# A state-space layer and expert mix on one core: y and B turned by VectorE, group factors copied by GpSimd

## What is computed

```python
proj = xn @ in_proj_w.T                       # gate (4096), x (4096), B, C (8*128 each), dt (64)
xBC  = silu(causal_conv(proj_xBC, 4 taps) + conv_bias)
# for every head: state = state*exp(dt*A) + (dt*x) B^T ;  y = state C
y    = y + x * D
yn   = y * rsqrt(mean(y*y over a group of 512) + eps) * norm_weight * silu(gate)
out  = x_in + yn @ out_proj_w.T + xn @ W_base.T + b_base + top2_lora(xn)
```

## Time and profile before

| | us |
|---|---|
| median of 3 runs | 3145.19 |
| lowest, highest | 3144.51, 3145.26 |
| profiled execution, device time | 3145.09 |
| its span in the trace | 3143.4 |

### The profile page before, as it was taken

The page is one execution under the profiler, slowest core; times in us unless marked ns, Lnnn a source line. Parts: engine busy times, 40 slices in busy tenths (PEclk is TensorE's granted clock), DMA queues, the critical chain, the costliest instruction groups (busy, mean ns, idle before and its releaser), DMA issues.

```text
span 3143.4 us, 55218 instructions
## 1 busy us (share of the span) xinstructions
PE 3126.1 (99%) x17660; PEld 2573.4 (82%) x17660; DVE 2558.5 (81%) x4599; ACT 1704.5 (54%) x4467; POOL 835.5 (27%) x917
## 2 busy tenths in 40 slices
...
GB/s 290 274 265 272 264 276 266 261 256 263 232 216 194 189 201 187 189 194 201 173 225 205 191 191 191 201 184 190 209 166 236 196 195 187 195 194 201 186 189 161
DMA packets 185668, 672.63 MB, mean 214 GB/s; under 512 B 21056, under 2 KB 22208, under 8 KB 185408
## 3 DMA queue, kind: packets, MB, share of 16 engines
...
...
## 4 chain that ended last, share of the span: by engine, by line
PE 95%; DVE 2%; ACT 1%; DMA 1%; issue 0%; SPq 0%; POOL 0%; ACTq 0%; DVEq 0%; POOLq 0%
PE dense L1072 21%; PE dense L1074 21%; PE dense L1073 21%; PE pX L1072 7%; PE pX L1074 7%; PE pX L1073 6%; PE pY L1187 3%; PE pD L1217 1%; PE pD L1187 1%; DVE conv_us L1497 1%; PE pCB L1163 1%; PE pU L1072 1%; PE pS L1073 1%; PE pS L1072 1%; PE pS L1074 1%; PE pU L1074 1%
## 5 line engine op out<-in xcount | busy, mean ns | idle before, releaser
L1072 PE MATMUL dense<-xn_hi,w_hl 128*128 128x512 f32 (+2 forms) x2192 | 869.7, 397 | 0.8 <-POOL w_hl L444 0.5
L1074 PE MATMUL dense<-xn_hi,w_hl 128*128 128x512 f32 (+2 forms) x2192 | 853.7, 389 | 0.0
L1073 PE MATMUL dense<-xn_lo,w_hl 128*128 128x512 f32 (+2 forms) x2192 | 852.0, 389 | 0.0
L1497 DVE SCALAR_TENSOR_TENSOR conv_us<-conv_in,const_g,conv_us 128x512 f32<-128x512 f32 x576 | 480.3, 834 | 47.0 <-ACT conv_us L694 33.2
L1074 PEld LDWEIGHTS dense<-xn_hi,w_hl 128*128 128x128 f32 (+1 forms) x2192 | 409.5, 187 | 88.9
L1072 PEld LDWEIGHTS dense<-xn_hi,w_hl 128*128 128x128 f32 (+1 forms) x2192 | 409.9, 187 | 86.0 <-issue 2.2
L1073 PEld LDWEIGHTS dense<-xn_lo,w_hl 128*128 128x128 f32 (+1 forms) x2192 | 410.3, 187 | 83.5 <-issue 1.2
L1072 PE MATMUL dense<-z_hi,w_hl 128*128 128x512 f32 x820 | 324.4, 396 | 1.6 <-DVE acc L1680 1.1
L501 POOL TENSOR_TENSOR C_lo<-BC,C_hi 128x128 fp32r<-128x128 f32 x120 | 60.0, 500 | 983.5 <-ACT S_hi L736 982.9
L1074 PE MATMUL dense<-z_hi,w_hl 128*128 128x512 f32 x820 | 319.7, 390 | 0.0
L1073 PE MATMUL dense<-z_lo,w_hl 128*128 128x512 f32 x820 | 319.1, 389 | 0.0
...
## 6 DMA issues: line engine op xcount, KB each, us to landing
...
cum_b<-cum_scratch ACTq DMA_DIRECT2D x128, 512.0 KB, 4.9
...
```

The costliest lines, as they stand in the source:

```text
L1072: nc.tensor.matmul(out, lhs[0], rhs[0], start=start, stop=False)
L1073: nc.tensor.matmul(out, lhs[0], rhs[1], start=False, stop=False)
L1074: return nc.tensor.matmul(out, lhs[1], rhs[0], start=False, stop=stop)
L1497: nc.vector.scalar_tensor_tensor(out=conv_u[r], in0=conv_in[r][:, t:t + TB], scalar=const_g[p][:, 4 * j + t:4 * j + t + 1], in1=conv_u[r], ...
```

## The change

The transposes of yn for chunks 2 and 3 go from PE to DVE: yn_rows, gated_pair and gated_lo_pair take the first chunk of the pair as a parameter, and chunk_3 stays only for group 0's last chunk. xT and BC become parts of one tile xBC, so x_rows turns B together with x (five tiles instead of four an instruction), and B_rows goes. chunk_1_x and chunk_1_cb of paired groups fall into wx_product, dtx_product, b_low and cb_masked; ACT's chunk_1 into b_high, cs_high, wx_high and ramps. conv_tap is one tap alone. prep of paired groups 2 to 7 moves to the start of GpSimd's list for the group, as products with ones. All four lists are in a new order.

```diff
 xn_lo = sb("xn_lo", [128, KD, TB], F32R)
 w_raw = [sb(f"w_raw{i}", [128, 1024]) for i in range(2)]
 w_hl = [sb(f"w_hl{i}", [128, 2, 2, 512], F32R) for i in range(2)]
-xT = [sb(f"xT{i}", [128, XT, TB]) for i in range(2)]
-BC = [sb(f"BC{i}", [128, 2, TB]) for i in range(2)]
+xBC = [sb(f"xBC{i}", [128, XT + 2, TB]) for i in range(2)]
...
                 ln_inv(q + 1, 3)
             lo(g, K_X + 8)
-    def paired_group(g, p, last=False):
+    def prep(g):
+        n = chunk(q, g - 1, NC - 1)
+        pool.wait_ge(y_s, carry_n(q, g - 1, NC - 1, first_block) + 1)
+        pool.wait_ge(xw_done, n * 2 + 2)
+        pool.wait_ge(relu_done, n * 2 + 2)
+        nc.gpsimd.tensor_tensor(tok_g[:], tok[:, :, g * HPG:(g + 1) * HPG],
+                                ones[:, 0:HPG].unsqueeze(1).broadcast_to([128, 5 * NC, HPG]), ALU.mult)
+        pool.wait_ge(xd_done, n + 1 + 1)
+        nc.gpsimd.tensor_tensor(D_g[:], D_all[:, g * HPG:(g + 1) * HPG], ones[:, 0:HPG], ALU.mult)
+        pool.wait_ge(evac_act, act_n(q, g - 1, 4 + NSET - 1))
+        nc.gpsimd.tensor_tensor(halo[:, g, :, :], halo_out[:], ones[:, 0:3].unsqueeze(1).broadcast_to([128, NSET, 3]), ALU.mult)
+        nc.gpsimd.tensor_tensor(halo_in[:], halo[:, g + 1, :, :], ones[:, 0:3].unsqueeze(1).broadcast_to([128, NSET, 3]), ALU.mult).then_inc(prep_done, 1)
+    def paired_group(g, p, second=True, last=False):
+        if second:
+            prep(g)
         chunk_pre(g, p, 0)
         wx_low(g, 0)
         chunk_pre(g, p, 1)
...
     gate_unit(0)
-    normalize(g - 1, 3, second)
+    if not second:
+        normalize(0, 3)
     gate_unit(1)
-    chunk_1(g, p, 0, last, two=True)
-    z_high(g - 1, 3)
+    cs_high(g, p, 0)
+    if not second:
+        b_high(g, 0, True)
+        wx_high(g, 0)
+        z_high(0, 3)
+    gate_unit(2)
+    ramps(g, 0, True)
+    next_cum(g, 0, last)
+    gate_unit(3)
+    if second:
+        b_high(g, 0, True)
+        wx_high(g, 0)
     skip(g, 0)
-    gate_unit(2)
-    gate_unit(3)
     skip(g, 1)
-    chunk_1(g, p, 1, last, two=True)
+    b_high(g, 1, True)
+    wx_high(g, 1)
+    cs_high(g, p, 1)
+    ramps(g, 1, True)
+    next_cum(g, 1, last)
     if last:
         router_copy()
     mean_square(g, 0, True)
     mean_square(g, 1, True)
-    def normalize_pair():
-        normalize(g, 0, True)
-        normalize(g, 1, True)
-    chunk_1(g, p, 2, last, two=True, behind_wx=normalize_pair)
+    b_high(g, 2, True)
+    cs_high(g, p, 2)
+    wx_high(g, 2)
+    normalize(g, 0, True)
+    normalize(g, 1, True)
+    ramps(g, 2, True)
+    next_cum(g, 2, last)
     skip(g, 2)
     if not last:
         x_unit(0)
         ev_conv(g, K_X + 1, 1, turn_bank(12 + 1), p)
         tanh_conv(g, 0)
-    chunk_1(g, p, 3, last, two=True)
+    b_high(g, 3, True)
+    cs_high(g, p, 3)
+    wx_high(g, 3)
+    ramps(g, 3, True)
+    next_cum(g, 3, last)
     skip(g, 3)
-    z_high_pair(g, p)
+    z_high_pair(g, p, 0)
     if not last:
         x_unit(2)
         x_unit(3)
-        x_unit(4)
     mean_square(g, 2, True)
     mean_square(g, 3, True)
+    normalize(g, 2, True)
+    normalize(g, 3, True)
     if last:
-        normalize(7, 2, True)
-        normalize(7, 3, True)
-        z_high(7, 2)
-        z_high(7, 3)
+        z_high_pair(7, 1, 2)
     else:
-        normalize(g, 2, True)
-        x_unit(5)
-        z_high(g, 2)
...
     gate_unit(g, False, 0, True)
-    if second:
-        chunk_3(g - 1, 2, two=True)
     gate_unit(g, False, 1, True)
+    gate_unit(g, False, 2, True)
+    if not second:
+        chunk_3(0, 3)
     chunk_1(g, 0, p, True, True)
-    gate_unit(g, False, 2, True)
-    chunk_3(g - 1, 3, two=second)
     gate_unit(g, False, 3, True)
+    out_units(g, 0, two=True)
     chunk_2s(g, 0)
     chunk_2b(g, 0)
-    out_units(g, 0, two=True)
+    out_units(g, 1, two=True)
     chunk_1(g, 1, p, True, True)
-    out_units(g, 1, two=True)
     if last:
         router_transpose()
     out_units(g, 2, two=True)
     chunk_2b(g, 3)
     chunk_2y(g, 2, True)
     chunk_2y(g, 3, True)
-    x_units(2)
-    if last:
-        chunk_3(7, 2, two=True)
-        x_units(1)
-        chunk_3(7, 3, two=True)
-        x_units(1)
+    x_units(4 if last else 2)
 group(0, 0, first=True)
 if first_block:
...
         for f in range(first, end):
             for k in range(4):
-                src = xT[p][32 * f:32 * f + 32, :, :].rearrange("n j (c t) -> n j c t", c=NC)
-                dst = x_tm[32 * k:32 * k + 32, :, :].rearrange("p c (j i) -> p j c i", j=XT)
+                src = xBC[p][32 * f:32 * f + 32, 0:XT + 1, :].rearrange("n j (c t) -> n j c t", c=NC)
+                dst = x_tm[32 * k:32 * k + 32, :, :].rearrange("p c (j i) -> p j c i", j=XT + 1)
                 ins = nc.vector.transpose(dst[:, :, :, 32 * f:32 * f + 32], src[:, :, c:c + 2, 32 * k:32 * k + 32])
         if end == 4:
             ins.then_inc(xt_done, 1)
-    def B_rows(g, p, first, end):
-        if first == 0:
-            dve.wait_ge(post, post_n(q, g, XT))
-            dve.wait_ge(ck_evac, chunk(q, g, 0))
-            dve.wait_ge(bl_done, chunk(q, g, 0))
-        for f in range(first, end):
-            for k in range(4):
-                src = BT[p][32 * f:32 * f + 32, :].rearrange("n (c t) -> n c t", c=NC)[:, :, 32 * k:32 * k + 32]
-                ins = nc.vector.transpose(B_tm[32 * k:32 * k + 32, :, 32 * f:32 * f + 32], src)
...
             ins.then_inc(yt_done, 1)
-    def gated_pair(g, p):
+    def gated_pair(g, p, c):
+        cs = slice(c * Q, (c + 2) * Q)
         dve.wait_ge(gate_done, grp(q, g) * XT + XT)
-        dve.wait_ge(yt_done, (q - 1) * (G - 1) + g)
-        z = xT[p][:, :, 0:2 * Q]
-        nc.vector.tensor_tensor(z, z, gate[:, :, 0:2 * Q], ALU.mult).then_inc(z_done, 2)
-    def gated_lo_pair(g, p):
-        dve.wait_ge(zhi_done, chunk(q, g, 0) + 2)
-        nc.vector.tensor_tensor(z_lo[:, :, 0:2 * Q], xT[p][:, :, 0:2 * Q],
-                                z_hi[:, :, 0:2 * Q].bitcast(F32), ALU.subtract).then_inc(z_done, 2)
+        dve.wait_ge(yt_done, yt_n(q, g, c))
+        nc.vector.tensor_tensor(xT[p][:, :, cs], xT[p][:, :, cs], gate[:, :, cs], ALU.mult).then_inc(z_done, 3)
...
     j_first = 1 if last else 0
-    x_rows(g, 0, p, 1 if second else 0, 4)
-    chunk_1_x(g, 0, True)
-    gated(g - 1, 3)
-    chunk_1_cb(g, 0, True)
-    gated_lo(g - 1, 3)
-    gate_tile(g, 0, False)
-    gate_tile(g, 1, False)
+    x_rows(g, 0, p, 0, 1)
+    if second:
+        silu(g - 1, 5, p)
+        gated_lo_pair(g - 1, 1 - p, 2)
+        x_rows(g, 0, p, 1, 2)
+        gate_tile(g, 0, False)
+        gate_tile(g, 1, False)
+        x_rows(g, 0, p, 2, 4)
+        wx_product(g, 0)
+        dtx_product(g, 0)
+        gate_tile(g, 2, False)
+        b_low(g, 0)
+    else:
+        x_rows(g, 0, p, 1, 4)
+        wx_product(g, 0)
+        gated(0, 3)
+        b_low(g, 0)
+        gated_lo(0, 3)
+        gate_tile(g, 0, False)
+        gate_tile(g, 1, False)
+        dtx_product(g, 0)
+        gate_tile(g, 2, False)
+    cb_masked(g, 0)
     masked(g, 0, True)
-    gate_tile(g, 2, False)
+    gate_tile(g, 3, False)
+    dve.wait_ge(acc_loaded, (q + 1) * 64)
+    out_adds(g, 0, halves=(0,), two=True)
     if last:
         router_weights()
+    out_adds(g, 0, halves=(1,), two=True)
     y_state(g, 0, True)
     y_skip(g, 0, True)
-    gate_tile(g, 3, False)
     state(g, 0)
-    dve.wait_ge(acc_loaded, (q + 1) * 64)
-    chunk_1_x(g, 1, True)
-    out_adds(g, 0, halves=(0,), two=True)
...
-    yn_rows(g, p, 0, 1)
+    yn_rows(g, p, 0, 0, 1)
     out_adds(g, 3, halves=(1,), two=True)
-    yn_rows(g, p, 1, 3)
+    yn_rows(g, p, 0, 1, 3)
     if last:
         x_unit(0)
-    yn_rows(g, p, 3, 4)
+    yn_rows(g, p, 0, 3, 4)
     masked(g, 2, True)
     if last:
         x_unit(1)
     y_state(g, 2, True)
     y_skip(g, 2, True)
     state(g, 2)
-    gated_pair(g, p)
+    gated_pair(g, p, 0)
     if not last:
         x_unit(0)
-    chunk_1_x(g, 3, True)
+    wx_product(g, 3)
+    dtx_product(g, 3)
     x_unit(j_first + 1)
-    chunk_1_cb(g, 3, True)
-    gated_lo_pair(g, p)
+    b_low(g, 3)
+    cb_masked(g, 3)
+    gated_lo_pair(g, p, 0)
     masked(g, 3, True)
-    if last and not last_block:
-        ln_stats(q + 1, 0)
-        ln_stats(q + 1, 1)
-    x_unit(j_first + 2)
-    x_unit(j_first + 3)
-    if last and not last_block:
-        ln_apply(q + 1, 0)
-        ln_apply(q + 1, 1)
-    y_state(g, 3, True)
-    y_skip(g, 3, True)
-    state(g, 3)
-    y_intra(g, 2, True)
-    y_intra(g, 3, True)
-    x_unit(j_first + 4)
-    if not last:
-        x_rows(g + 1, 0, 1 - p, 0, 1)
-    x_unit(j_first + 5)
-    if not last:
-        B_rows(g + 1, 1 - p, 0, 2)
-    gated(g, 2)
-    gated_lo(g, 2)
     if last:
+        if not last_block:
+            ln_stats(q + 1, 0)
+        x_unit(3)
+        y_state(g, 3, True)
+        y_skip(g, 3, True)
+        state(g, 3)
+        y_intra(g, 2, True)
+        y_intra(g, 3, True)
+        if not last_block:
+            ln_stats(q + 1, 1)
```

(55 more changed lines are left out.)

166 lines of the change are left out of this document (102 added, 64 removed).

## The result

| | us |
|---|---|
| after, median of 4 runs | 3206.49 |
| lowest, highest | 3204.48, 3208.88 |
| before, median | 3145.23 |
| ratio after / before, 95% interval | 1.0195 [1.0177, 1.0213] |
| span of the profiled execution after | 3207.1 |

The change costs 61.3 us, where the prediction said 26 and its range ended at 3203. The direction and the mechanism were as forecast, the size was not.

What follows compares the result with a forecast made beforehand. PE bounded the kernel before; DVE's loop was to bound paired groups after. Blocks 1 and 2 +25.8, last block +6.6, slack -3, transposes outside -3: total +26, 3171 us, range 3122 to 3203.

Steps and rivals of the forecast that it cites:

- PE as bound before, and its saving: PE bounds the kernel before; yn transposes leaving save 0.49 us a chunk, group 88.05 to 87.1 (last block 86.4).
- Work of DVE, +3.6 to 82.6: Per paired group, added yn transposes and wider x transposes, less B transposes and prep, raise DVE's unhidden work to 82.6 us.
- Waits: DVE's waits on ACT and GpSimd per group: 5.1 us before; some go, and a new 1.25 precedes the second yn transposes.
- Lengthened instructions: DVE instructions slowed beside GpSimd's SBUF reads: 4.0 us a group before; z_lo's 0.7 and chunk 1 B_lo's 0.5 go.
- four possible meetings: New DVE and GpSimd overlaps at a group's start, 0.85 us each, 0 to +3.4; one taken, 1.0.
- L: DVE's own loop over a paired group, work plus unavoidable waits and lengthening: forecast 90.2 us, bounds 89.2 and 92.6.
- Block 3: In the last block chunk 3 has no state update, so L is 1.7 us shorter: 88.5 against 87.4 before.
- the slack once a block: PE's slack before ACT's masked ramps of chunk 3, used up once in each of three blocks: -3 us.
- PE stays the bound: Rival: DVE's waits and lengthening fit into 4.5 us a group; full gain, 3124.5 us; chance 0.28.
- the draw: Rival: L about 88.5, each group's PE gain lost again on DVE; 3139 to 3151 us; chance 0.12.
- GpSimd's prep coming late: Rival: late prep holds C_lo, S_lo and products, costing 1 us a group, 3163 us; contained in case 3.
- case 3: The forecast itself: DVE's loop bounds the paired groups, 3151 to 3215 us; chance 0.60.

Runs made afterwards that it cites:

- all_orders: Changed kernel with gate_order's move, half of chunk 3's first yn transposes and the pair's gate product behind wx and dtx, and a later constants' copy: 3131.3 us.
- gate_order: Changed kernel with DVE's order at a group's start altered: more x transposes before the gate tiles, chunk 0's masked ramps before gate tile 2 and B_lo: 3169.0 us.
- before_plus_6: Kernel before with six unused 512-element reductions added on DVE in every paired group, PE's list untouched: 3207.9 us.
- before_prep_pool: Kernel before with only prep of paired groups 2 to 7 moved to GpSimd: 3145.2 us.
- half_second_turn: Changed kernel with only 8 of the 16 yn transposes of chunks 2 and 3 done, the rest left out: 3154.8 us.

## Why the prediction came out as it did

**PE as bound before, and its saving.** Right. Per chunk 0.49 and a group of 87.1 (86.4 in block 3) are what all_orders shows where nothing else holds PE, 87.2 and 86.44.

**Work of DVE, +3.6 to 82.6.** Right: 82.9 measured. The ten-block transpose was put at 503 ns; the group of these instructions over the whole span (count | busy us, mean ns | idle before) reads

```profile
L1576 DVE STREAM_TRANSPOSE x_tm<-xBC 32x320 f32<-32x320 f32 x672 | 337.7, 503 | 13.9 <-DVE B_lo L1595 1.0
```

**Waits.** Forecast 1.3 before the first yn transposes, 1.25 before the second, 1.26 before the pair's z_lo: 3.8. Measured 0.78, 1.20 and 0.98, and 0.41 before a B_lo that the sum did not have: 3.4. The new wait was sized to 0.05 us. That the total came near is in part luck: 0.8 too much at two of the places against the 0.4 that was missing.

**Lengthened instructions: here the step failed.** Forecast 4.0 - 1.2 + 1.0 = 3.8, measured 5.4. The prediction listed four possible meetings (two gate tiles, B_lo with wx_lo, the constants' copy with the state of chunk 1), priced each at 0.85 and took one. Three of them, the two gate tiles with S_lo and S_cur, and B_lo with wx_lo, happen in the same way in every paired group but a block's first, at 1.3 together and 1.1: 2.4 instead of 1.0. The price was good enough, 3 x 0.85 = 2.55; the number of meetings was not. gate_order removes just these and gets 2.4 back. The other 0.2 of the 5.4 is B_lo of chunk 3, 1.1 against the 0.9 carried over. "Which happen depends on tenths" was true, and the conclusion wrong: tenths decide once, and then it is the same in each of the groups, since the starts in DVE's loop repeat to some 0.02 us. It should have been laid out in time. The prediction put C_lo 2.5 behind silu(5) (here 1926.84 - 1924.02 = 2.8); C_lo, S_lo and S_cur take 2.8 together, so they end 5.3 behind it. Silu, z_lo and four transposes take 0.6 + 1.2 + 2.1 = 3.9, so the gate tiles had to fall into the last 1.4 of GpSimd's run.

**The copy of the constants** is the fourth meeting. It takes 1.04 instead of 0.29 in one group each of blocks 1 and 2, while S_cur runs beside it. That group lasts 92.8, 1.1 more than the others. (In one group of block 3 it takes 0.58, and the group 90.9.) DVE of after in order of time, then GpSimd:

```profile
2036.92 2.05 DVE L1576 STREAM_TRANSPOSE x_tm<-xBC 32x320 f32<-32x320 f32 x4 [0.49 <-DVE B_lo L1595]
2038.99 1.04 DVE L1751 TENSOR_SCALAR const_g<-consts 128x34 f32<-128x34 f32 x1
...
2038.95 1.04 POOL L512 TENSOR_TENSOR S_cur<-S_cur,tok_g 128x512 f32<-128x512 f32 x1
```

**DVE's loop before.** L was taken apart from 88.05, as if PE and DVE were level, and before_plus_6 puts DVE's own loop at 87.55. This did no harm: the 0.5 between them is B_lo of chunk 1, which the prediction had among what goes. Counted from 87.55 the loop was forecast to grow by 2.65 and grew by 4.1, short by the same 1.5. "None is a wait on PE" was not quite so: that B_lo was held by wx_lo, which came round at PE's 88.08. It shrank to 0.28 as soon as DVE came later, and grew to 1.29 in before_prep_pool, where DVE came earlier.

**Block 3.** Forecast 1.7 shorter than the others, measured 1.1 (90.57). The state's two products are gone (1.2), and of the lengthening at chunk 3 another 1.7, but DVE comes to the pair's z_lo sooner and waits there. Its row in block 3 of after, against 0.98 in block 2:

```profile
2782.89 1.22 DVE L1726 TENSOR_TENSOR z_lo<-xBC,z_hi 128x1024 fp32r<-128x1024 f32 x1 [2.83 <-ACT z_hi L829]
```

The prediction had said that ACT's chain bounds this spot, and yet took off the work as if nothing came back. The kernel before already showed it: in its block 3 the same z_lo waits 2.91, where block 2 has 1.26.

**The sum with measured terms.** Blocks 1 and 2: 12 x (91.67 - 88.05) = 43.4, and one group in each with the copy, 2 x 1.1 = 2.2. Block 3: 6 x (90.57 - 87.40) = 19.0. That is 64.6; the total of 61.3 leaves -3.3 for the slack once a block and the transposes outside, forecast as -6; this rest was not taken apart. Of the 35 us that were missing, 12 x 1.47 = 17.6 and 6 x 2.07 = 12.4 come from L, 2.2 from the copy, and 2.7 from this rest.

**The rivals.** 1 (PE stays the bound, 3124.5; with half of the waits hidden 3125 to 3138) is what all_orders comes near to at 3131.3. Its argument, that half of 6.5 us of waits and lengthening might be hidden, was not absurd: with three moves on DVE it nearly holds. As the change was written it doesn't. 2, the draw, would need L at 88.5, which is near where half_second_turn stands. 4, GpSimd's prep coming late, is excluded by before_prep_pool. The upper bound of case 3, 3215, held the result; cutting the range at 3203 did not.
